# A chunked recurrence in which two small factors reach all partitions by a store and a broadcast load instead of by TensorE transposes

## The reference, cut to what matters

```python
def step(S, t):
    q_t, k_t, v_t, a_t, b_t = t
    y = jnp.einsum('bhvk,bhk->bhv', S, k_t)
    err = y - v_t
    S = a_t[..., None] * S - (b_t[..., None] * err)[..., None] * k_t[:, :, None, :]
    o = jnp.einsum('bhvk,bhk->bhv', S, q_t)
    return (S, o)
...
mu = jnp.mean(o, axis=-1, keepdims=True)
var = jnp.mean(jnp.square(o - mu), axis=-1, keepdims=True)
o = (o - mu) * jax.lax.rsqrt(var + LN_EPS) * ln_g + ln_b
g = jax.nn.sigmoid(x @ Wg).reshape(b, t, H, D)
o = (o * g).reshape(b, t, H * D)
return o @ Wo
```

## Time and profile before

| | |
|---|---|
| median of three runs | 3097.45 us (3096.15 to 3103.75) |
| span of the profiled execution | 3102.6 us |
| mean granted TensorE clock | 0.976 of full speed |
| recurrence, 32 chunks | 636 to 2755 us |
| PE busy | 2732.2 us (88%) |
| DVE busy | 2239.8 us (72%) |
| ACT busy | 1610.3 us (52%) |
| POOL busy | 1377.8 us (44%) |

### The profile page before, as it was taken

One profiled execution on the slowest core, in us unless ns is written; L12 is line 12 of the kernel. 1 busy time (PEld: TensorE's weight loads), 2 busy tenths in 40 slices (PEclk: granted clock), 3 DMA queues, 4 the chain that ended last, 5 costly groups with the idle time before them and its releaser, 6 DMA issues. The chain is left out here.

```text
span 3102.6 us, 48417 instructions
## 1 busy us (share of the span) xinstructions
PE 2732.2 (88%) x14144; PEld 1863.5 (60%) x14144; DVE 2239.8 (72%) x4680; ACT 1610.3 (52%) x3516; POOL 1377.8 (44%) x1760
## 2 busy tenths in 40 slices
PE   7999999768898888988889888898888888859999
PEld 3555555446666666666666666666666666635555
DVE  6777777677888878888788887888887888623332
ACT  6666666545555555555555555555555555412111
POOL 3666676734544445444454444544445444310000
PEclk9999999989999999999999999999999999979999
DMA  3655556533232232322323223232223222034120
GB/s 124 241 225 206 233 230 239 196 82 67 43 57 42 44 65 47 57 42 43 64 49 57 42 44 59 53 57 42 44 51 61 46 53 43 9 107 109 45 38 14
DMA packets 449883, 261.22 MB, mean 84 GB/s; under 512 B 402672, under 2 KB 414672, under 8 KB 447472
## 3 DMA queue, kind: packets, MB, share of 16 engines
q1 hardware_dynamic: 449664, 258.51, 31.5%
HBM read 153.42 MB, written 105.05 MB: 83 GB/s over the span
## 5 line engine op out<-in xcount | busy, mean ns | idle before, releaser
L265 DVE SCALAR_TENSOR_TENSOR A_acc<-A_psY,A_w,A_acc 128x410 f32<-128x410 f32 (+1 forms) x720 | 419.2, 637 | 151.6 <-ACT A_acc L334 151.6
L405 PE MATMUL A_psY<-A_xT,A_w 128*128 128x413 f32 (+1 forms) x960 | 347.2, 510 | 9.1 <-PE A_psAG L411 7.7
L1244 ACT ACTIVATE B_PQ<-B_psM 128x64 f32<-128x64 f32 (+2 forms) x480 | 125.2, 261 | 441.2 <-DVE B_NC L1137 440.9
L1137 DVE TENSOR_TENSOR B_NC<-B_NC,B_psM 128x256 f32<-128x256 f32 x480 | 200.8, 418 | 182.5 <-PE B_psM L1756 92.8
L192 POOL TENSOR_TENSOR A_outs<-A_outs,A_acc 128x410 f32<-128x410 f32 (+1 forms) x240 | 229.7, 987 | 216.1 <-ACT A_outs L342 216.1
L899 POOL TENSOR_TENSOR B_WT<-B_WT,B_G 128x128 f32<-128x128 f32 (+2 forms) x224 | 143.4, 640 | 371.2 <-ACT B_WT L1244 184.3
L1244 ACT ACTIVATE B_WL<-B_psT 64x128 f32<-64x128 f32 (+3 forms) x480 | 148.5, 309 | 265.6 <-PE B_psT L1723 265.4
L405 PEld LDWEIGHTS A_psY<-A_xT,A_w 128*128 128x128 f32 x960 | 180.2, 189 | 165.5 <-issue 164.2
L1140 DVE TENSOR_REDUCE B_W<-B_NC 128x64 f32<-128x320 f32 x512 | 248.7, 486 | 17.6
L334 ACT ACTIVATE A_acc<-A_psY,A_w 128x410 f32<-128x410 f32 (+1 forms) x240 | 166.1, 692 | 162.9 <-PE A_psY L405 161.2
L879 POOL TENSOR_TENSOR B_PQ<-B_PQ,B_G 128x256 f32<-128x256 f32 x128 | 89.4, 699 | 345.5 <-DVE B_WT L1105 345.5
(11 more groups left out here) (207 smaller groups left out, 6588.4 us busy)
## 6 DMA issues: line engine op xcount, KB each, us to landing
B_KQ<-scr SPq DMA_DIRECT2D x96, 512.0 KB, 6.6
scr<-A_outs SPq DMA_DIRECT2D x48, 615.0 KB, 3.5
scr<-A_outag SPq DMA_DIRECT2D x32, 615.0 KB, 5.2
scr<-A_outs SPq DMA_DIRECT2D x48, 409.0 KB, 2.5
A_xc<-nbeta SPq DMA_DIRECT2D x16, 1024.0 KB, 5.9
B_A<-scr SPq DMA_DIRECT2D x32, 512.0 KB, 4.6
B_C<-scr SPq DMA_DIRECT2D x32, 512.0 KB, 6.3
B_G<-scr SPq DMA_DIRECT2D x32, 512.0 KB, 4.6
```

The lines of the kernel that those rows point to most:

```text
L265: nc.vector.scalar_tensor_tensor(a, y, w[:, s, col:col + 1], a, ALU.mult, ALU.add)\
L405: last = nc.tensor.matmul(psY[p][:, y0:y0 + HALO + t1 - t0], wp[:, p, kt, :], xT[:, kt, t0:t1 + HALO], start=kt == 0, stop=kt == KT - 1)
L1137: tt(eq[:, :, :, 1:5], eq[:, :, :, 1:5], left.unsqueeze(2).to_broadcast([128, H, R, R]), ALU.mult)\
L1244: copy = lambda out, in_: nc.scalar.activation(out, in_, ACT.Copy)
```

## The change

The decays are no longer spread by PE. SP stores `Gs[4]` to a tensor `decay` of 16 x 128 numbers in memory (2048 single numbers of 4 bytes) and loads that back to all 128 partitions (1 MB) into the tile `B_WX`, once the outputs of chunk g - 1 are centred (ACT, step 8), since `B_WX` is used until then. `decay_state` reads both operands from SBUF, and its four instructions stand in steps 11, 12, 15 and 15. The deviations are inverted in place where they lie (8 partitions x 128), stored (4 KB) and loaded back to all partitions (512 KB) into `B_SQ`; `norm` reads them there. The jobs `decay`, `dev` and `rstd` leave PE's list, and with them 25 transposes a chunk. `deviation` moves on ACT from step 12 to step 11, ahead of `pairs_copy`, and `invert` on DVE from step 13 to step 12. In `project_inputs` three semaphores that release a buffer of weights become one that counts three.

```diff
-        7: [("decay", 0)] + ([("oc_rest", 1)] if out else []),
+        7: ([("oc_rest", 1)] if out else []),
         8: ([("own", 0, 1)] if not last else []),
-        9: [("decay", 1)],
         10: ([("kk", 0, 0), ("kk", 0, 1)] if not last else []) + ([("var", 0)] if out else []),
         11: ([("wo", 0)] if wo else []),
-        12: ([("gram", 0)] if not last else []) + ([("dev", 0)] if out else []) + ([("wo_rest", 0)] if wo else []),
-        13: [("decay", 2), ("decay", 3)],
-        14: [("ktok", 1)] + ([("rstd", 0)] if out else []) + ([("wo_rest", 1)] if wo else []) + ([("rstd", 1)] if out else []),
+        12: ([("gram", 0)] if not last else []) + ([("wo_rest", 0)] if wo else []),
+        14: [("ktok", 1)] + ([("wo_rest", 1)] if wo else []),
...
+            def store_decays(g):
+
+                wait(sp, g4, g, 1)
+                wait(sp, dld, g, 0)
+                sp.dma_start(decay_d.rearrange("h v -> v h"), Gs[4][:].rearrange("p h j -> p (h j)"), allow_slow_non_contiguous=True)\
+                  .then_inc(dst.sem, 16)
+
+            def load_decays(g):
+
+                wait(sp, dst, g + 1, 0)
+                wait(sp, oc, g, 0)
+                sp.dma_start(WXF, decay_d.rearrange("h v -> (h v)").partition_broadcast(128)).then_inc(dld.sem, 16)
+
+            def spread_rstd(o):
+
+                wait(sp, rd, o, 1)
+                wait(sp, rld, o, 0)
+                sp.dma_start(rstd_d, sdev[:]).then_inc(rst.sem, 16)
+                wait(sp, rst, o, 1)
+                sp.dma_start(FQ, rstd_d.rearrange("i x -> (i x)").partition_broadcast(128)).then_inc(rld.sem, 16)
...
             for g in range(NCH):
                 at, n = (g + 1) * C, (g + 1) % 2
+                store_decays(g)
...
+                load_decays(g)
+                if g:
+                    spread_rstd(g - 1)
                 if g % 2 and g >= 3:
                     store((g - 3) // 2)
...
-                ps = take_bank(dve, g, "decay", i)
+                wait(dve, dld, g, 1)
                 x = ST[:, 4 * i:4 * i + 4, :]
-                tt(x, x, ps[:].rearrange("p (h v) -> p h v", h=4), ALU.mult).then_inc(stg.sem, 1)
+                tt(x, x, GB[:, 4 * i:4 * i + 4, :], ALU.mult).then_inc(stg.sem, 1)
...
                     elif j == 10:
-                        decay_state(g, 0)
                         mask_gram(g, 5)
                     elif j == 11:
-                        decay_state(g, 1)
+                        decay_state(g, 0)
                         if more:
                             row_pairs(nxt)
                             leaf_solution(nxt, 1)
                     elif j == 12:
+                        if g:
+                            invert(g - 1)
+                        decay_state(g, 1)
                         if more:
                             leaf_solution(nxt, 2)
                     elif j == 13:
-                        if g:
-                            invert(g - 1)
...
                     elif j == 11:
+                        if g:
+                            deviation(g - 1)
                         if more:
                             pairs_copy(nxt)
```

More of the change, by code:

```diff
@@ L103, in project_inputs @@
         w_ld = [Count(sem(f"A_w_ld{s}"), 1, 16) for s in range(2)]
-        w_used = [Count(sem(f"A_w_used{s}"), 1, 1, 1) for s in range(2)]
-        c_used = [Count(sem(f"A_c_used{s}"), 1, 1, 1) for s in range(2)]
-        ca_used = [Count(sem(f"A_ca_used{s}"), 1, 1, 1) for s in range(2)]
+        w_used = [Count(sem(f"A_w_used{s}"), 3) for s in range(2)]
         y_full = [Count(sem(f"A_y_full{p}"), 2 * NTA) for p in range(3)]
@@ L246, in _ @@
                 tap[p].start(dve)
-            c_used[0].start(dve)
-            c_used[1].start(dve)
             with dve.Fori(0, TURNS) as t:
@@ L315, in _ @@
             nc.scalar.activation(nbeta[:], beta[:], ACT.Copy, scale=-SCALE * SCALE).then_inc(nbeta_sb, 1)
-            for c in (*ag_free, *ca_used):
+            for c in ag_free:
                 c.start(act)
@@ L390, in _ @@
             pe.wait_ge(beta_sb, T // 512)
-            w_used[0].start(pe)
-            w_used[1].start(pe)
             with pe.Fori(0, TURNS) as t:
@@ L460, in chunk_jobs @@
     if g == NCH:
-        return [("qk", n, l) for n in range(3) for l in range(2)] + [("oc", 0), ("oc", 1), ("var", 0), ("dev", 0), ("rstd", 0), ("rstd", 1)]
+        return [("qk", n, l) for n in range(3) for l in range(2)] + [("oc", 0), ("oc", 1), ("var", 0)]
     if g > NCH:
@@ L517, in recurrence @@
         sem = lambda name: ctx.enter_context(nc.semaphore("B_" + name))
+        decay_d = nc.dram_tensor("decay", (H, D), FP32).ap()
+        rstd_d = nc.dram_tensor("rstd", (8, 128), FP32).ap()
         wo = sb("wo", [128, H, HID])
@@ L647, in taken @@
                 return (am if n else atc, (g - 3) // 2, 1),
-            return {"contact": (cont, g, n + 1), "ktok": (ktok, g, n + 1), "decay": (stg, g, n + 1),
+            return {"contact": (cont, g, n + 1), "ktok": (ktok, g, n + 1),
                     "update": (stu, g, n + 1), "oc": (oc, g - 1, n + 1),
-                    "var": (sd, g - 1, 1), "dev": (rd, g - 1, 1), "rstd": (on, g - 1, n + 1)}[kind],
+                    "var": (sd, g - 1, 1)}[kind],
         def open_bank(pe, *job):
@@ L752, in _ @@
             load("G", 0, T - C)
+            spread_rstd(NCH - 1)
             store(NCH // 2 - 1)
@@ L757, in _ @@
                 loaded(sp, what, NCH - 1)
+            wait(sp, dst, NCH, 0)
+            wait(sp, dld, NCH, 0)
+            wait(sp, rst, NCH, 0)
+            wait(sp, rld, NCH, 0)
             wait(sp, ldc, NCH, 0)
@@ L808, in block_decays @@
                 wait(pool, dec, g, DEC)
-                wait(pool, stg, g, 0)
+                wait(pool, dst, g, 0)
                 wait(pool, psc, g, 0)
@@ L836, in decayed_w @@
                 wait(pool, oc, o - 1, 2)
+                wait(pool, stg, o + 1, 0)
                 for r in range(3):
@@ L848, in decayed_q @@
                 wait(pool, mq0, o + 1, 0)
-                wait(pool, sd, o - 1, 1)
+                wait(pool, on, o - 1, 2)
                 tt(FQ.rearrange("p (r l h n) -> p r l h n", r=R, l=2, h=H)[:, n], by_row(Qs[o % 2])[:, n],
@@ L1063, in invert @@
             def invert(o):
-                ps = take_bank(dve, o + 1, "dev", 0)
-                nc.vector.reciprocal(rdev[:], ps[:, 0:8]).then_inc(rd.sem, 1)
+                wait(dve, sd, o, 1)
+                nc.vector.reciprocal(sdev[:], sdev[:]).then_inc(rd.sem, 1)
             def norm(o, i):
-                ps = take_bank(dve, o + 1, "rstd", i)
+                wait(dve, rld, o, 1)
                 x = O[:, 8 * i:8 * (i + 1), :]
-                tt(x, x, ps[:].rearrange("p (h c) -> p h c", h=8), ALU.mult).then_inc(on.sem, 1)
+                tt(x, x, SQ[:, 8 * i:8 * (i + 1), :], ALU.mult).then_inc(on.sem, 1)
             def att_sum(u):
@@ L1376, in w_rows_copy @@
                 wait(act, ws, o + 1, 0)
+                wait(act, stg, o + 1, 0)
                 copy(as_rows(WX[:])[:, 0:7:2], by_row(W[:])).then_inc(wxc.sem, 1)
@@ L1502, in chunk @@
                             block_keys(nxt)
-                        if g:
-                            deviation(g - 1)
                         if more:
@@ L1595, in shared_job @@
                         last = nc.tensor.transpose(ps[:, 128 * m:128 * (m + 1)], KQ[:, s, 0, 2 * i:2 * i + 2, :].rearrange("p h c -> p (h c)"), ident[:])
-                elif kind == "decay":
-                    wait(pe, g4, g, 1)
-                    for m in range(4):
-                        last = nc.tensor.transpose(ps[:, 128 * m:128 * (m + 1)],
-                                                   Gs[4][:, 4 * n + m, :].to_broadcast([128, 128]), ident[:])
                 elif kind == "oc":
@@ L1613, in shared_job @@
                                   start=i == 0, stop=i == 7)
-                elif kind == "dev":
-                    wait(pe, sd, g - 1, 1)
-                    last = nc.tensor.transpose(ps[:, 0:8], sdev[:], ident[0:8, 0:8])
-                elif kind == "rstd":
-                    wait(pe, rd, g - 1, 1)
-                    for m in range(4):
-                        i = 4 * n + m
-                        last = nc.tensor.transpose(ps[:, 128 * m:128 * (m + 1)],
-                                                   rdev[:, i:i + 1].to_broadcast([128, 128]), ident[:])
                 elif kind == "wo":
```

16 lines of the change are left out of this document (9 added, 7 removed).

## The result

The changed kernel takes 3275.36 us (median of 4 runs, 3241.31 to 3290.82) against 3098.11 us: a ratio of 1.0532, with a 95% interval from 1.0479 to 1.0585. The forecast was 3139 us with a range of 3108 to 3168. The direction was right, the size was not: +177 us instead of +42. (The ratio is that of the mean times, without the execution of 3290.82 us, which counts as slow; by it the change costs 165 us. Both figures carry the spread of 50 us between the changed kernel's executions.)

A forecast was written before the change was run, and what follows sets the result against it. It took the chain DVE, PE, ACT, PE round each step as the bound. Pairs of chunks add 2.48 us, 37 us over 15, plus 5 at the tail: span 3145, median 3139 us, range 3108 to 3168.

The forecast's parts named there:

- what is taken off PE: 25 transposes a chunk, about 2.8 us of PE: worth nothing, except 0.88 us at the end of odd chunks.
- the clock: Rival: PE less busy, every even chunk gets a half-speed stretch (mean 0.95); +30 us, 3169 us; chance 0.05.
- `row_pairs` held by the root: Step 11: ACT's copy into B_X waits for the square root, row_pairs start 2.09 us later, step 12 1.40 later.
- Step 12: DVE gets reciprocal, decay multiplication and GpSimd wait: grows 1.15 us (0.83 to 2.23), partly in earlier idle time.
- the bound by the slope: Step 12's reciprocal on DVE, at 5.8 ns an element: 0.9 us instead of the 0.23 taken.
- A half wait: Step 12: DVE's wait for GpSimd's SBUF reads, taken as 0.32 us between no wait and two waits.
- Step 13 and the odd end: Step 13 loses the reciprocal: -0.12 us even, -0.12 and -0.17 (at step 14) odd; odd chunk's end -0.88.
- An odd chunk's terms: Net growth of an odd chunk, after idle time and the shorter end: 0.39 us.
- an even one's: Net growth of an even chunk: 1.40 + 0.81 - 0.12 = 2.09 us.
- All hidden: New stores and loads of decays and reciprocals cost nothing, except after the last chunk; decays' load hidden by 1 to 3 us.
- The tail: After the last chunk, a store and a load replace 1.27 us and 0.3 us of transpose: +5 us.

The follow-up runs named there:

- b_decay_dma: The kernel before with only the decays sent by store and broadcast load, deviations and reciprocals still through PE: 3161.21 us, ratio 1.0187 to the kernel before.

## Why the prediction was wrong, step by step

- **The step that failed: what is taken off PE is "worth nothing".** The prediction asked only whether the transposes stood on the path, and found that PE waits for DVE anyway. Those waits were the problem: the transposes filled them and kept the clock. Taking 16 away costs 63 us, and putting useless ones in their place brings all of it back. Among the rivals the clock stood at a chance of 0.05 and +30 us, as one stretch at 0.95 in every even chunk; it came as 10 to 24 us of half clock in every even one and 6 in the mean odd one. The row of 64.96 us had shown what such a stretch costs. "Only few chunks have one now" was a wrong reading of the trace, too: 9 of the 15 even chunks of before had one, so the kernel already stood at the edge.
- **Its size.** 352 us more of half clock at the 0.28 us each that a fit over the even chunks of before gives make some 98 us; with the fits over the changed kernel's own chunks, 0.31 (even) and 0.45 (odd), some 120. The rest of the 177 goes by the terms below, in steps at full clock: (2.45 + 0.68) x 15 = 47, the store 26, the tail 6. (The store's 26 holds some half clock too, so this is rough; by either fit the clock is over half.)
- **`row_pairs` held by the root: right.** 1.89 us of idle (2.09 forecast), step 11 +1.18 (1.40 forecast), alone 29 us.
- **Step 12: mis-sized, inside its bounds.** Even +1.37 (+0.81 forecast), odd +0.73 (+0.16 forecast). The reciprocal of 128 numbers a partition is 0.93 us, 0.87 without overlap; I took 0.23, and the bound by the slope (0.9) was right. The decay multiplication was not held (0.62); GpSimd's meeting hit L1050 behind it (1.06 against 0.60), and POOL's own L906 took 1.79 us for 0.80. A half wait, 0.32, was near the 0.46.
- **Step 13 and the odd end: right.** -0.10 and -0.35 (-0.12, -0.29); the end 7.29 to 6.41, -0.88 as computed. An odd chunk's terms sum to +0.68 (+0.39 forecast), an even one's at full clock to 2.45 (2.09).
- **"All hidden": wrong for the store.** The decays' load, yes: no row of DVE waits for it. But the store of 2048 numbers stood ahead of the loads in SP's order, which then took 14.0 us; the prediction looked only at the next chunk, which the loads serve, and overlooked that GpSimd reads A early in it. 26 us, measured in the changed kernel with fillers; in b_decay_dma step 6 grew by 0.1 us only.
- **The tail: right in size, partly by luck.** From the last update to the first `norm` 27.4 us instead of 21.6, +5.8 (+5). Only 3.6 us of that lie behind the root, from whose end to `norm` it takes 5.50 us and not 1.90: the load is issued 1.2 us after the store (1.7 forecast) and there some 3.3 us later (5). The other 2.2 us come ahead of the root. DVE after the last chunk:

```profile
2897.32 0.94 DVE L1092 RECIPROCAL B_E<-B_E 8x128 f32<-8x128 f32 x1 [16.95 <-ACT B_E L1420]
2902.79 1.29 DVE L1097 TENSOR_TENSOR B_O<-B_O,B_SQ 128x512 f32<-128x512 f32 x2 [4.53 <-DMA B_SQ<-rstd]
```

Taken one at a time the causes come to 63 (decay transposes) + 42 (reciprocals by transfer) + 29 (root) + 26 (store) = 160 of 177 us. They don't add strictly, since waiting in one place adds half clock in others. How the clock's cost divides between places inside a chunk stays open beyond steps 10, 11 and the end.

## What to carry to other kernels

When a kernel runs at nearly full clock with short pauses on PE, price the removal of PE's work by what it does to the clock: take the work out and put useless work of the same length in its place; if the times differ, the saving was a cover. Replace matmuls by transfers only where they stand on the path, and see that the new transfer is made of long pieces and stands behind the loads that others wait for. After shortening one stretch, look for DVE and GpSimd instructions that now start together.
